# A vision layer on one core: DVE's normalisation split in two and moved, and the mixture's row transposes given to DMA

## The reference, cut to what matters

```
h = concat([cls, patches @ W_lin.T + b_lin])                 # (64, 197, 192)
x = _layernorm(h);  q, k, v = split(x @ qkv_weight.T)        # 12 heads of 16
q = _layer_norm(q) * SCALE;  k = _layer_norm(k)              # per head
h = h + (softmax(q @ k.T) @ v) @ proj_weight.T
x = _layernorm(h)
scores = sigmoid(x @ gate_weight.T)                          # 8 experts, 4 groups, 2 chosen
y = sum over experts e of cw[e] * (silu(x @ w1[e].T) * (x @ w3[e].T)) @ w2[e].T
z = (silu(x @ sw1.T) * (x @ sw3.T)) @ sw2.T                  # a ninth, shared expert
h = h + y + z
```

## Time and profile before

| | us |
|---|---|
| median of 2 runs | 1719.84 (1719.72 to 1719.96) |
| the profiled execution, its own time | 1721.13 |
| its span, first to last instruction | 1719.3 |
| PE busy | 1622.7 (94%) |
| DVE busy | 1274.5 (74%) |
| ACT busy | 1010.0 (59%) |
| POOL busy | 602.2 (35%) |

### The profile page before, as it was taken

One profiled execution on the slowest core, in us unless ns is written; L12 is line 12 of the kernel. 1 busy time (PEld: TensorE's weight loads), 2 busy tenths in 40 slices (PEclk: granted clock), 3 DMA queues, 4 the chain that ended last, 5 costly groups with the idle time before them and its releaser, 6 DMA issues. The chain is left out here.

```text
span 1719.3 us, 44326 instructions
## 1 busy us (share of the span) xinstructions
PE 1622.7 (94%) x16914; PEld 1124.4 (65%) x16914; DVE 1274.5 (74%) x3660; ACT 1010.0 (59%) x2089; POOL 602.2 (35%) x658
## 2 busy tenths in 40 slices
PE   5999999999999999999998499999999999999998
PEld 4777777777777777777776255555555555555555
DVE  5677777666666666666664488888888888888887
ACT  2777776666666666666666345445454545455452
POOL 2333333333333333333331143343434343343433
PEclk8999999999999999999999699999999999999999
DMA  7233333333333333333310100001010100001000
GB/s 236 68 76 76 76 76 76 76 77 76 76 76 77 76 77 78 77 78 78 79 35 12 35 29 27 31 19 38 20 38 20 34 24 29 29 20 38 16 20 16
DMA packets 40863, 95.19 MB, mean 55 GB/s; under 512 B 4491, under 2 KB 17454, under 8 KB 40526
## 3 DMA queue, kind: packets, MB, share of 16 engines
q1 hardware_dynamic: 31438, 72.89, 13.6%
q0 software_dynamic: 9216, 19.47, 7.5%
HBM read 92.44 MB, written 19.37 MB: 65 GB/s over the span
## 5 line engine op out<-in xcount | busy, mean ns | idle before, releaser
L1343 POOL TENSOR_TENSOR in_lo<-inner,in_hi 128x512 f16<-128x512 f32 (+1 forms) x225 | 257.3, 1144 | 434.1 <-ACT act L1130 434.1
L885 POOL CAST qk_strips<-qk_norm 99x768 f16<-99x768 f32 x128 | 106.8, 835 | 606.3 <-DVE qk_norm L754 606.3
L589 ACT ACTIVATE prob<-ps_sc 99x792 f32<-99x792 f32 x384 | 302.5, 826 | 2.6 <-PE ps_sc L404 2.6
L1138 ACT ACTIVATE in_hi<-inner 128x512 f16<-128x512 f32 (+1 forms) x225 | 140.3, 624 | 181.2 <-DVE inner L1258 181.2
L1130 ACT ACTIVATE act<-ps_h 128x512 f32<-128x512 f32 (+1 forms) x225 | 131.7, 586 | 189.8 <-PE ps_h L1056 189.8
L1276 DVE SCALAR_TENSOR_TENSOR acc<-ps_y,comb,acc 128x192 f32<-128x192 f32 (+1 forms) x700 | 241.8, 407 | 0.3 <-PE ps_y L1072 0.3
L1258 DVE SCALAR_TENSOR_TENSOR inner<-ps_h,act 128x512 f32<-128x512 f32 (+1 forms) x225 | 153.6, 683 | 103.5 <-ACT act L1130 99.9
L1070 PE MATMUL ps_y<-w_hi,in_hi 128*128 128x192 f16 (+1 forms) x900 | 223.9, 249 | 3.7 <-DVE acc L1276 1.9
L1072 PE MATMUL ps_y<-w_hi,in_lo 128*128 128x192 f16 (+1 forms) x900 | 221.4, 246 | 0.0
L1071 PE MATMUL ps_y<-w_lo,in_hi 128*128 128x192 f16 (+1 forms) x900 | 221.4, 246 | 0.0
L342 PE MATMUL ps_hid<-lin_hi,x_hi 128*99 128x192 f16 x768 | 194.7, 254 | 18.9 <-DVE x_lo L701 10.4
(11 more groups left out here) (157 smaller groups left out, 3802.6 us busy)
## 6 DMA issues: line engine op xcount, KB each, us to landing
xin<-xp SPq DMA_DIRECT2D x64, 594.0 KB, 4.3
x_hi<-xp POOLq DMA_DIRECT2D x64, 297.0 KB, 4.0
hidden_dram<-h SPq DMA_DIRECT2D x64, 147.0 KB
hin<-hidden_dram SPq DMA_DIRECT2D x24, 384.0 KB, 3.1
out<-acc SPq DMA_DIRECT2D x24, 384.0 KB, 2.4
w_f<-w SPq DMA_DIRECT2D x1, 2304.0 KB, 9.2
hidden_dram<-h SPq DMA_DIRECT2D x64, 0.8 KB
w_f<-w SPq DMA_DIRECT2D x1, 864.0 KB, 11.2
```

Source lines behind the costliest of these rows:

```text
L589: act.activation(prob[quad][:, places].rearrange("p h m s -> p h (m s)"), ps_sc[0:TR, places, 0:2 * SLOTS], ACT.Exp, scale=D ** -0.5 / (SQ ...
L1343: pool.tensor_tensor(in_lo[b][:, 0:N], inner[b][:, 0:N], in_hi[b][:, 0:N], ALU.subtract).then_inc(inlo_done, 1)
```

## The change

**In the attention part** `norm_hidden(n1)` becomes two calls, one for each t. The first stays where it was, the second goes behind `v_copy(n2)`, and `o_out(n4, 0)` goes ahead of `qk_normalise(n2, 1)`. PE's transposes of `xnorm` wait for both halves.

**In the mixture part** the PE transposes and both `yT_out` go. ACT's `normalise` writes `bnorm` without the doubled columns (two instructions a half) and then its float16 first part `y_hi` (two more); POOL's new `rest_of` writes the remainder `y_lo` (two a half); SP's new `transposes` issues four DMA transposes a half (float16, 128 rows by 256 columns, from SBUF to SBUF) into `yT_hi` and `yT_lo`, which get a third buffer. This is done two groups ahead instead of one: `normalise` at e = 5 and 6, `rest_of` at e = 6 and 7, `rstds` at e = 3 (5 before), `stats_of` at e = 1 and 2 (2 and 4 before); `gate` comes at e = 3 (4 before), and DVE's route parts 0 to 3 at e = 4, 5, 6 and 8 (5 to 8 before). The next `normalise` waits until the transposes of the group before it have landed, since `y_hi` has one buffer. The factor 64 that `yT_out` applied moves into `rstds`.

```
-                    pe.wait_ge(xnorm_done, n2.times(1, 1))
+                    pe.wait_ge(xnorm_done, n2.times(2, 2))
...
-            def norm_hidden(n):
...
-                for t in range(2):
-                    dve.tensor_scalar(xnorm[:, t, 0:C], h[n.mod(HB)][:, t, :], meanvar[:, t, 0:1],
-                                      h_rstd[:, t:t + 1], ALU.subtract, ALU.mult)
-                    last = dve.tensor_scalar(xnorm[:, t, C:256], h[n.mod(HB)][:, t, 128:C], meanvar[:, t, 0:1],
-                                             h_rstd[:, t:t + 1], ALU.subtract, ALU.mult)
-                last.then_inc(xnorm_done, 1)
+            def norm_hidden(n, t):
+                if t == 0:
+                    dve.wait_ge(hrstd_done, n.times(1, 1))
+
+                    if reached(n.times(1)):
+                        dve.wait_ge(xT_done, n.times(1))
+                dve.tensor_scalar(xnorm[:, t, 0:C], h[n.mod(HB)][:, t, :], meanvar[:, t, 0:1],
+                                  h_rstd[:, t:t + 1], ALU.subtract, ALU.mult)
+                dve.tensor_scalar(xnorm[:, t, C:256], h[n.mod(HB)][:, t, 128:C], meanvar[:, t, 0:1],
+                                  h_rstd[:, t:t + 1], ALU.subtract, ALU.mult).then_inc(xnorm_done, 1)
 
...
                     qk_variance(n2, 1)
                 if n1.active():
-                    norm_hidden(n1)
-                if n2.active():
-                    qk_normalise(n2, 1)
-
+                    norm_hidden(n1, 0)
                 if n4.active():
                     o_out(n4, 0)
                 if n2.active():
+                    qk_normalise(n2, 1)
                     v_copy(n2)
+                if n1.active():
+                    norm_hidden(n1, 1)
                 if k.back(-1).active():
                     split(k.back(-1), 0)
...
-        bnorm = sb("bnorm", [128, T, 256])
-        yT_hi = [sb(f"yT_hi{p}", [128, 2, GT], F16) for p in range(2)]
-        yT_lo = [sb(f"yT_lo{p}", [128, 2, GT], F16) for p in range(2)]
+        bnorm = sb("bnorm", [128, T, C])
+        y_hi = sb("y_hi", [128, T, 256], F16)
+        y_lo = sb("y_lo", [128, T, 256], F16)
+        yT_hi = [sb(f"yT_hi{p}", [128, 2, GT], F16) for p in range(3)]
+        yT_lo = [sb(f"yT_lo{p}", [128, 2, GT], F16) for p in range(3)]
...
-        ps_x = [ps(f"ps_x{k}", [128, 512]) for k in range(2)]
+        ps_gate = ps("ps_gate", [128, 512])
...
+            def transposes(g, half_no):
+                R, p = rows_of(g), g.mod(3)
+                sp.wait_ge(ylo_done, g.times(2, half_no + 1))
+                if half_no == 0 and reached(g.times(NE, -2 * NE)):
+                    sp.wait_ge(inner_done, g.times(NE, -2 * NE))
+                for t in (2 * half_no, 2 * half_no + 1):
+                    s = slice(t * R, (t + 1) * R)
+                    sp.dma_start_transpose(yT_hi[p][:, :, s], y_hi[0:R, t, :]).then_inc(yT_in[p], 16)
+                    sp.dma_start_transpose(yT_lo[p][:, :, s], y_lo[0:R, t, :]).then_inc(yT_in[p], 16)
...
+            for g in range(2):
+                transposes(Index(0, g, 2, GROUPS_B), 0)
+                transposes(Index(0, g, 2, GROUPS_B), 1)
 
...
+                ahead = g.back(-2)
                 if g.back(-3).active():
                     load(g.back(-3))
+                if ahead.active():
+                    transposes(ahead, 0)
+                    transposes(ahead, 1)
                 store(g)
...
-            def transposes(g):
-                R = rows_of(g)
-                pe.wait_ge(bnorm_done, g.times(2, 2))
+            def gate(g):
+                R, p = rows_of(g), g.mod(3)
+                pe.wait_ge(yT_in[p], 32 * T * (g.c // 3 + 1))
 
                 if reached(g.times(1)):
                     pe.wait_ge(tanh_done, g.times(1))
                 for t in range(T):
                     s = slice(t * R, (t + 1) * R)
-                    for k in range(2):
-                        last = pe.transpose(ps_x[k][:, s], bnorm[0:R, t, k * 128:(k + 1) * 128], id32[0:R, 0:R])
-                last.then_inc(yT_done, 1)
...
-                N, p, b = T * rows_of(g), g.mod(2), (g.c + e) % 2
-                if e == 0:
-                    pe.wait_ge(yThi_done, g.times(2, 2))
-                    pe.wait_ge(yTlo_done, g.times(2, 2))
-
+                N, p, b = T * rows_of(g), g.mod(3), (g.c + e) % 2
...
-                    if e == 2 and following.active():
-                        transposes(following)
-                    if e == 4 and following.active():
+                    if e == 3 and following.active():
                         gate(following)
...
+                ts = slice(2 * half_no, 2 * half_no + 2)
                 act.wait_ge(bneg_done, g.times(1, 1))
+                if reached(g.times(2, half_no - 1)):
+                    act.wait_ge(ylo_done, g.times(2, half_no - 1))
+                for t in (2 * half_no, 2 * half_no + 1):
+                    last = act.activation(bnorm[0:R, t, :], hin[p][0:R, t, :], ACT.Identity,
+                                          scale=brstd[0:R, t:t + 1], bias=bshift[0:R, t:t + 1])
+                last.then_inc(bnorm_done, 1)
+                act.wait_ge(bnorm_done, g.times(2, half_no + 1))
+
                 if half_no == 0 and reached(g.times(1)):
-                    act.wait_ge(yT_done, g.times(1))
-                for t in (2 * half_no, 2 * half_no + 1):
-                    for dst, src in ((slice(0, C), slice(0, C)), (slice(C, 256), slice(128, C))):
-                        last = act.activation(bnorm[0:R, t, dst], hin[p][0:R, t, src], ACT.Identity,
-                                              scale=brstd[0:R, t:t + 1], bias=bshift[0:R, t:t + 1])
-                last.then_inc(bnorm_done, 1)
-
-            def yT_out(g):
-                N, p = T * rows_of(g), g.mod(2)
-                act.wait_ge(yT_done, g.times(1, 1))
-                for k in range(2):
-                    act.activation(yT_hi[p][:, k, 0:N], ps_x[k][:, 0:N], ACT.Copy,
-                                   scale=SX).then_inc(yThi_done, 1)
+                    before = g.back(1)
+                    act.wait_ge(yT_in[before.mod(3)], 32 * T * (before.c // 3 + 1))
+                act.activation(y_hi[0:R, ts, 0:C], bnorm[0:R, ts, :], ACT.Copy)
+                act.activation(y_hi[0:R, ts, C:256], bnorm[0:R, ts, 128:C], ACT.Copy).then_inc(yhi_done, 1)
 
...
+            second = first.back(-1)
             normalise(first, 0)
             normalise(first, 1)
-            yT_out(first)
+            normalise(second, 0)
+            normalise(second, 1)
             gate_out(first)
...
+                following, ahead = g.back(-1), g.back(-2)
                 for e in range(NE):
                     silu(g, e)
                     inner_first(g, e)
-                    if e in (0, 1) and following.active():
-                        normalise(following, e)
-                    if e == 2 and following.active():
-                        yT_out(following)
-                    if e == 4 and following.active():
+                    if e in (5, 6) and ahead.active():
+                        normalise(ahead, e - 5)
+                    if e == 3 and following.active():
                         gate_out(following)
...
-                    if e in (2, 4) and ahead.active():
-                        stats_of(ahead, e // 2 - 1)
-                    if e == 3 and following.active():
-                        yT_out(following)
-                    if e > 4 and following.active():
-                        route(following, e - 5)
+                    if e in (1, 2) and ahead.active():
+                        stats_of(ahead, e - 1)
+                    if e in (4, 5, 6) and following.active():
+                        route(following, e - 4)
+                    if e == 8 and following.active():
+                        route(following, 3)
...
                 pool.wait_ge(bmv_done, g.times(T, T))
                 settle(pool, settled)
-                pool.tensor_scalar(bvareps[0:R], bmv[0:R, :, 1], EPS, None, ALU.add).then_inc(bve_done, 1)
+                pool.tensor_scalar(bvareps[0:R], bmv[0:R, :, 1], EPS, 1.0 / SX ** 2,
+                                   ALU.add, ALU.mult).then_inc(bve_done, 1)
...
+            def rest_of(g, half_no):
+                R = rows_of(g)
+                ts = slice(2 * half_no, 2 * half_no + 2)
+                pool.wait_ge(yhi_done, g.times(2, half_no + 1))
+                pool.tensor_tensor(y_lo[0:R, ts, 0:C], bnorm[0:R, ts, :], y_hi[0:R, ts, 0:C], ALU.subtract)
+                pool.tensor_tensor(y_lo[0:R, ts, C:256], bnorm[0:R, ts, 128:C], y_hi[0:R, ts, C:256],
+                                   ALU.subtract).then_inc(ylo_done, 1)
...
+            first, second = Index(0, 0, 2, GROUPS_B), Index(0, 1, 2, GROUPS_B)
+            rstds(first)
+            rest_of(first, 0)
+            rest_of(first, 1)
+            rstds(second)
+            rest_of(second, 0)
+            rest_of(second, 1)
...
                     inner_rest(g, e)
```

(14 more changed lines are left out.)

30 lines of the change are left out of this document (9 added, 21 removed).

## The result

| | before | after |
|---|---|---|
| median, us | 1719.84 | 1693.05 (1692.76 to 1693.34) |
| ratio to before, 95% interval | | 0.984 [0.9812, 0.9869] |
| span of the profiled execution | 1719.3 | 1690.9 |

What follows compares the result with a forecast made beforehand. The prediction took PE's own stream to set the end. From the profiled execution, 1721.13 - 16 (attention) - 19.7 + 2 (steady mixture) + 2.6 (filling) = 1690.0, less 1.3 to the median: 1689 us, range 1668 to 1712.

Steps and rivals of the forecast that it cites:

- Attention, -16: Attention part: moving `o_out(n4, 0)` ahead gains 0.26 us an image, 62 x 0.26 = 16 us less; bounds 0 and 40.
- 0.26 of the 0.61: Attention part: L388 starts 0.61 us earlier, but L404 waits for ACT's fourth exponential, so 0.26 an image is gained.
- Rival (b): Attention part: POOL and DVE block each other, L887 between the two `xnorm`; +5 instead of -16, 1710; chance 0.17.
- The 1.4: Attention part: DVE held 1.4 us if L887 also got between the two `xnorm` instructions, PE 0.35 late; called possible.
- the cover: Attention part: slack behind DVE's later work; holds up to 1.05 us of further DVE delay, beyond that each 0.1 costs 6.
- Steady, -19.7 + 2: Mixture part, steady groups: PE's transposes gone, 19.7 us less; 2 us lost to the late chain at e = 5 to 8.
- Filling, +2.6: Filling of the mixture part: first `gate` 2.1 us later, later `multiply`, less the second group's transposes; 2.6 more, bounds 0 and 8.
- the third row: Span table, first `gate` to second and last `gate` to the end: forecast +0.5 us.
- sign that the transposes land within 2 us: Mixture part: expected evidence for the forecast, `gate` without a wait for DMA and DMA transposes landing within 2 us.
- Rival (a): Mixture part: DMA transposes too slow, PE waits at `gate`; decides at 1.6 us a transfer, 1960 at 3.1; chance 0.14.
- Rival (c): Mixture part: PE waits for `in_lo` or `acc` at e = 8, 0.4 to 0.9 a group, 1698 to 1710; chance 0.10.
- Rival (d): Attention part: whole 0.61 to 0.65 gained as ACT's exponentials move up too; 24 less, 1665; chance 0.09.

## Why the prediction was right, and where it was not

- **Attention, -16: -17.7, and -17.2 by itself.** 0.26 of the 0.61 reach the end, as worked out, and the rest turned into L404's wait. The undone split and the moved exponential show that ACT is the limit. The 1.2 to 1.7 beyond the forecast are about the 1.5 of chance.
- **Rival (b), POOL and DVE blocking each other.** Half of it is there: L734 of the second half takes 0.62 instead of 0.37, beside POOL's cast, so it is held 0.25 and not the 0.5 that the prediction took as certain. The 1.4 is not there: L736's median is 307 ns, and two of 128 reach 1.0 us. POOL's L886 behind it takes up to 1.72 and nobody waits for it. DVE still idles 0.46 ahead of `o_out(n4, 1)`, of the 0.7 worked out, so the cover held.
- **Steady, -19.7 + 2: -17.35.** The transposes' price is right to 0.01: with the remainders off POOL the period is 28.81, which is 29.68 less 0.87. The 2 us of loss is right in size (2.3) and wrong in cause, so that part of the agreement is luck. I looked for it in ACT's longer blocks (worked out as 1.76, and 1.72 in the trace, 1274.81 to 1276.53); they are the same with the remainders on DVE, where nothing is lost. The loss goes with `rest_of` on POOL, where I counted only whether POOL keeps up. Half of it is a `multiply` that DVE starts out of a wait instead of out of work; at most 0.8 is POOL and DVE blocking each other, which I had counted in the attention part and not here; the 0.38 of the shorter long group is unexplained.
- **Filling, +2.6: +6.7.** This is the term that was mis-sized. I bounded a transfer between 0.5 and 3.1 and took up to 1.0, "for a small transfer". It is 1.29 for each, since SP is held by the instruction and not by the bytes, so the nearest row by size, the load of 384 KB, said nothing on it. With "four transfers landing, 3.1 as bound" and 1.5 for the queue, I reckoned as if they ran beside each other; the last lands 7 x 1.29 + 2.4 = 11.4 after the first starts. That is 5.2 too little up to the first gate, more than the whole error of 4.1; the merged transfers gave back 5.0. The blocks for the second group ahead of `gate_out` delay the first `multiply` by 2.5, as the sum had it but for its size (1.4 net, with no table load in it), and still the third row came out 1.1 better than forecast. The prediction's sign that the transposes land within 2 us failed too: it is 2.4.
- **Rival (a), transfers too slow.** 1.29 is below the 1.6 from which it decides, and `gate` doesn't wait after filling. But only 0.07 to 1.5 us were left: one pair more made the kernel 2% slower than the one before the change. (The Trainium skill, VectorE: DVE Perf Modes, "The three transpose paths", has 1309 ns for a block of 128x128. The estimate from it, by the block, was 20.9 us a group; the measurement decides, and it is 1.25 to 1.27 us for an instruction of two blocks or of four.)
- **Rival (c)** came at most as the two long groups, and in the longer alone PE is seen to wait, 0.61 for `acc`. **Rival (d)** asked for an earlier exponential; the change has none, and with one it was 14 us more.

The errors of the attention part (-1.7), of filling (+4.1) and of the steady part (+0.3) make 2.7 of span. This profiled execution stood 1.0 nearer to its median than the one before, and its own time is 2.4 above its span where it was 1.8, another 0.6: together 4.3, the distance from the sum's 1688.7 to 1693.05.

## What to carry to other kernels

Where a wait is taken away, look at once for the next operand of the same stream that is late: here the gain was 0.26 of 0.63, and an edit of one line on another engine gave another 0.22. Price a DMA transpose by the instruction on the queue that issues it, give each as much data as fits, and count the whole series where a pipeline fills, since nothing hides it there. Where such a series is hidden, read the margin in every group and not in one: it was 1.3 in the group that was read and 0.07 in the tightest. When work goes to GpSimd, ask what VectorE does with two inputs from SBUF at that moment, and not only whether GpSimd has time. Work that is hidden on VectorE can stay there: moving it off gained nothing here.

## What the runs showed of the hardware

- A DMA transpose, float16, SBUF to SBUF, holds SyncE 1.25 us (128x256) or 1.27 (128x512), and the next starts 0.04 later; it lands 2.4 or 2.5 after its start in the median. In the changed kernel 14 of 200 hold SyncE 1.6 to 2.4, and single ones land up to 4.5 after their start.
- A `TENSOR_TENSOR` with two SBUF inputs, 128x256 float32, takes VectorE 0.42 us, and up to 1.37 beside GpSimd's `TENSOR_TENSOR`. The same remainder of 128x384 takes 0.92 on GpSimd and 0.56 on VectorE.
- TensorE's clock: in the changed kernel it is at 0.50 after the wait of 26 us ahead of the first `gate`, and 512-column matmuls start 0.43 apart until 967.4. With the extra pair, 8 waits of PE of 1.96 to 2.91 us in otherwise full work came with a stretch at the lower level, which cost 1.3 to 1.7 us in seven of them (in the eighth, where PE also waits 0.62 for `acc`, 2.4). Three of 2.14 to 2.38 and the 13 shorter ones did not.
- ACT loads a function table for 1.28 us ahead of the tanh and again ahead of the next `silu` (`ACT_TABLE_LOAD`, 965.40 and 966.91 in the changed kernel).
